# The maximum pass of the last graph attention layer: source terms fetched as bf16 parts and laid under the targets by selector products

## The reference, cut to what matters

```python
def _L3_gnn_ref(feat, src, dst, W, attn_l, attn_r):        # n = 3125, HEADS = 4, OUT_DIM = 64
    ft = (feat @ W.T).reshape(n, HEADS, OUT_DIM)
    a1 = jnp.einsum('nhd,hd->nh', ft, attn_l)
    a2 = jnp.einsum('nhd,hd->nh', ft, attn_r)
    e = jax.nn.leaky_relu(a1[src] + a2[dst], negative_slope=ALPHA)
    m = jax.ops.segment_max(e, dst, num_segments=n)
    ex = jnp.exp(e - m[dst])
    s = jax.ops.segment_sum(ex, dst, num_segments=n)
    a = ex / s[dst]
    msg = ft[src] * a[:, :, None]
    return jax.nn.elu(jax.ops.segment_sum(msg, dst, num_segments=n).reshape(n, HEADS * OUT_DIM))
```

## Time and profile before

| | |
|---|---|
| median of the runs | 6750.23 us (3 runs, 6729.89 to 6758.26) |
| the profiled execution's own time | 6752.3 us |
| its span | 6750.5 us |
| granted TensorE clock over the span | 0.812 |
| busy share PE, PEld, DVE, ACT, POOL | 69%, 45%, 57%, 32%, 51% |
| first and last gather of the maximum pass | 5400.6 and 6036.2 us |

### The profile page before, as it was taken

How to read it: one execution, slowest core, us unless ns; L and a number is a source line. 1 busy time by engine, 2 the same in 40 slices (tenths; PEclk the granted TensorE clock), 3 DMA queues, 4 the chain that set the end, 5 groups by cost and what they waited for, 6 DMA issues and landing times. The chain is left out here.

```text
span 6750.5 us, 92101 instructions
## 1 busy us (share of the span) xinstructions
PE 4675.7 (69%) x21663; PEld 3026.9 (45%) x21663; DVE 3880.6 (57%) x14947; ACT 2148.6 (32%) x7478; POOL 3474.4 (51%) x3739
## 2 busy tenths in 40 slices
PE   3566674747895555638767774778778478888858
PEld 3223333737882222424345553555567233336635
DVE  8676543130016666351578877777532667778875
ACT  0000000212231222302344444444223188874421
POOL 3636665446635666456556663666122166656610
PEclk9776656869996776955689997999788699989978
DMA  1133335546745666013155555777456166664410
GB/s 47 48 98 91 91 92 159 185 143 218 232 149 151 181 181 175 14 45 103 49 151 162 148 145 152 237 237 236 133 150 170 45 173 171 172 154 141 140 44 20
DMA packets 526133, 916.95 MB, mean 136 GB/s; under 512 B 100305, under 2 KB 382880, under 8 KB 517168
## 3 DMA queue, kind: packets, MB, share of 16 engines
q0 software_dynamic: 170800, 477.35, 26.0%
q1 hardware_dynamic: 294378, 305.07, 14.5%
q10 hardware_dynamic: 60438, 128.64, 6.0%
HBM read 739.33 MB, written 171.37 MB: 135 GB/s over the span
## 5 line engine op out<-in xcount | busy, mean ns | idle before, releaser
L999 PE MATMUL bank<-small 128*125 128x256 f32 x1660 | 763.2, 587 | 472.3 <-DVE small L966 239.9
L947 POOL DMA_INDIRECT small<-tabA,idxD x830 | 809.9, 976 | 441.0 <-issue 187.2
L999 PEld LDWEIGHTS bank<-small 128*125 128x125 f32 x1660 | 368.1, 268 | 866.6 <-issue 469.5
L978 DVE TENSOR_TENSOR big<-big,bank 125x256 f32 x830 | 347.1, 418 | 490.4 <-PE bank L999 312.6
L2506 POOL DMA_INDIRECT small<-tabC,idxD x415 | 394.5, 951 | 343.2 <-issue 124.5
L2559 PE MATMUL bank<-small 128*125 128x512 f32 x830 | 474.6, 656 | 127.1 <-issue 104.0
L2548 ACT ACTIVATE small<-cst,small 128x128 f32<-128x128 f32 x1660 | 532.2, 388 | 94.0 <-issue 40.0
L1342 DVE COPY small<-bank 128x256 f32<-128x256 f32 x176 | 74.5, 424 | 834.5 <-PE bank L1382 423.2
L2277 POOL DMA_INDIRECT big<-tabB,idxD x415 | 394.6, 951 | 300.1 <-PE bank L2340 133.6
L2091 POOL DMA_INDIRECT small<-tabT,idxS x415 | 396.5, 955 | 284.5 <-PE bank L1989 141.2
L781 POOL DMA_INDIRECT recs<-pkS,rowS x391 | 383.8, 982 | 249.4 <-issue 100.2
(11 more groups left out here) (463 smaller groups left out, 11371.0 us busy)
## 6 DMA issues: line engine op xcount, KB each, us to landing
small<-eaS SPq DMA_DIRECT2D x830, 128.0 KB
big<-in_L_w ACTq DMA_DIRECT2D x56, 1024.0 KB
eaS<-small SPq DMA_DIRECT2D x415, 128.0 KB
big<-in_L2f_w ACTq DMA_DIRECT2D x64, 512.0 KB
ytab<-small ACTq DMA_DIRECT2D x176, 128.0 KB
big<-rowsS SPq DMA_DIRECT2D x52, 256.0 KB
small<-rowsD SPq DMA_DIRECT2D x52, 256.0 KB
small<-tabA,idxD POOLq DMA_INDIRECT x830
```

The source lines that it names most:

```text
L947: g.indirect_dma_start(out=self.gb[k % self.RG], out_offset=None, in_=K.tabA, in_offset=row_index(K.idxD, k)).then_inc(*self.got.up(k))
L978: v.tensor_tensor(rows, rows, K.bank[k % 4][0:PT, 0:D], ALU.add).then_inc(*self.added.up)
L999: p.matmul(self.K.bank[k % 4][0:PT, 0:D], self.oh[k % self.RO][:, 0:PT], self.gb[k % self.RG], start=True, stop=True).then_inc(*self.summe ...
```

## The change

The four source terms of a node no longer reach the maximum pass as fp32 numbers to be spread on diagonals. `L3Project` splits each into three bf16 parts whose sum is the fp32 number, and puts these 12 parts in 6 extra columns (PW = 6) ahead of the features, in the same rows. It does so in five batches of five node tiles (`part`, four dependent VectorE operations a batch); SyncE now waits for the batch (`parted`) instead of for the node tile (`stored`), so that the stores of `tabC` go out five at a time. The rows of `tabC` grow from 260 to 266 numbers. `L3Project` also builds a constant `sel` once: for head h it is 1 in rows h, h+4 and h+8, in 128 columns.

In the maximum pass TensorE transposes the first 128 bf16 columns of the gathered rows (L2590 of the new code). Rows 0 to 11 of the result are the parts of the 128 edges; ScalarE copies these 12 rows to `rowT` (L2580), whose other rows were zeroed once. Four bf16 products of 128 columns with `sel` (L2600) lay the sum of a head's three parts under every target, on top of the product of `no` with 1e30 (L2597), which now comes first. The mask `oh` and the diagonals are gone. ScalarE still puts the a1 aside (L2581). Banks 0 to 4 are now a ring of five for the products, banks 5 to 7 one of three for the transposes; `no` is a ring of five, `rowT` one of three. GpSimd waits for `taken` in place of `spread`. The number of gathers (415) and of feature writes (415) stays.

The diff:

```diff
--- before.py
+++ after.py
@@ -136,7 +136,7 @@
-        self.tabC = self.dram("tabC", [N, AW])
+        self.tabC = self.dram("tabC", [N, CW])
@@ -2393,6 +2393,8 @@
 AW = D + 4
 WA = D + 8
+PW = 6
+CW = PW + AW
 class L3Project(Project):
@@ -2401,8 +2403,12 @@
     def __init__(self, K):
         W, g = K.W, K.g
         K.w_at = K.g_at = 0
-        self.acc, self.ft = W(T * AW), W(T * WA)
-        self.a12, self.am = self.ft.rearrange("p (t c) -> p t c", c=WA)[:, :, D:WA], W(T * 8)
+        self.acc, self.ft = W(T * AW), W(T * (PW + WA))
+        self.ftv = self.ft.rearrange("p (t c) -> p t c", c=PW + WA)
+        self.a12, self.am = self.ftv[:, :, PW + D:PW + WA], W(T * 8)
+        self.left = W(T * 4)
+        self.sel = W(256, BF16)
+        self.sel1 = W(4)
         self.am3 = W(T * 12, BF16)
         self.A1 = W(EP * 4)
         self.identB = W(64, BF16)
@@ -2417,6 +2423,7 @@
         self.t_w, self.t_wn, self.t_at = K.ticket(), K.ticket(), K.ticket()
         super().__init__(K, T)
         self.attn, self.joined = K.mark(1), K.mark(1)
+        self.parted = K.mark(T // 5)
         self.tabs = K.ring(4, T)
     def sync(self, s):
@@ -2425,8 +2432,8 @@
         load(s, self.t_wn, self.wn, a["L3_Wn"])
         load(s, self.t_at, self.bd, a["L3_attn"])
         for t in range(T):
-            s.wait_ge(*self.stored.n(t + 1))
-            s.dma_start(K.tabC[t * PT:(t + 1) * PT, :], self.ft[0:PT, t * WA:t * WA + AW]).then_inc(*self.tabs.up(t))
+            s.wait_ge(*self.parted.n(t // 5 + 1))
+            s.dma_start(K.tabC[t * PT:(t + 1) * PT, :], self.ftv[0:PT, t, 0:CW]).then_inc(*self.tabs.up(t))
         for t in range(T - 4, T):
             s.wait_ge(*self.tabs.n(t))
@@ -2445,9 +2452,31 @@
         for h in range(4):
             v.tensor_scalar(self.bigI4[:, h * 128:(h + 1) * 128], K.ident, BIG, None, ALU.mult)
         v.memset(self.acc[0:PT, :], 0.0)
+        v.tensor_tensor(self.sel1, K.ident[:, 0:4], K.ident[:, 4:8], ALU.add).then_inc(*own.up)
+        v.wait_ge(*own.all)
+        v.tensor_tensor(self.sel1, self.sel1, K.ident[:, 8:12], ALU.add).then_inc(*own.up)
+        v.wait_ge(*own.all)
+        v.tensor_copy(self.sel.rearrange("p (h e) -> p h e", h=4), self.sel1.unsqueeze(2).broadcast_to([128, 4, 128]))
         self.stats.vector(v)
-        for t in range(T):
-            self.normalize(v, t)
+        for t in range(T + 4):
+            if t < T:
+                self.normalize(v, t)
+            if t >= 8 and t % 5 == 3:
+                self.part(v, t // 5 - 1)
+
+    def part(self, v, b):
+        own, ts = self.K.own_v, slice(5 * b, 5 * b + 5)
+        a1 = self.ftv[0:PT, ts, PW + D:PW + AW]
+        parts = self.ft.bitcast(BF16).rearrange("p (t c) -> p t c", c=2 * (PW + WA))[0:PT, ts, 0:12]
+        left = self.left.rearrange("p (t h) -> p t h", h=4)[0:PT, ts, :]
+        v.wait_ge(*self.stored.n(5 * b + 5))
+        v.tensor_copy(parts[:, :, 0:4], a1).then_inc(*own.up)
+        v.wait_ge(*own.all)
+        v.tensor_tensor(left, a1, parts[:, :, 0:4], ALU.subtract).then_inc(*own.up)
+        v.wait_ge(*own.all)
+        v.tensor_copy(parts[:, :, 4:8], left).then_inc(*own.up)
+        v.wait_ge(*own.all)
+        v.tensor_tensor(parts[:, :, 8:12], left, parts[:, :, 4:8], ALU.subtract).then_inc(*self.parted.up)
     def scalar(self, a):
         K = self.K
@@ -2457,7 +2486,7 @@
                 t = i - 2
                 p = K.bank[2 + t % 2][0:PT, 0:WA]
                 a.wait_ge(*self.product.n(t + 1))
-                a.activation(self.ft[0:PT, t * WA:(t + 1) * WA], p, ACT.Copy).then_inc(*self.stored.up)
+                a.activation(self.ftv[0:PT, t, PW:PW + WA], p, ACT.Copy).then_inc(*self.stored.up)
             if i < T:
                 self.turn(a, i)
@@ -2485,52 +2514,56 @@
 class L3Max:
-    RG = 8
+    RG, RT, RN = 8, 3, 5
     def __init__(self, K, proj):
         self.K, self.pr = K, proj
         g = K.g
         K.w_at, K.g_at = proj.w_end, 0
-        self.oh, self.no = [g(128) for _ in range(4)], [g(64, BF16) for _ in range(4)]
-        self.dg, self.tm = [g(512) for _ in range(4)], [g(4) for _ in range(4)]
-        self.gb = [g(AW) for _ in range(self.RG)]
+        self.no = [g(64, BF16) for _ in range(self.RN)]
+        self.tm = [g(4) for _ in range(4)]
+        self.rowT = [g(64, BF16) for _ in range(self.RT)]
+        self.gb = [g(CW) for _ in range(self.RG)]
         self.got, self.kept_rows = K.ring(self.RG, NTE, "gather"), K.ring(self.RG, NTE)
-        self.oneh, self.spread, self.field, self.top, self.kept = (K.mark(NTE) for _ in range(5))
+        self.empty = K.mark(1)
+        self.hole, self.flipped, self.turned, self.taken, self.field, self.top, self.kept = (K.mark(NTE) for _ in range(7))
     def gpsimd(self, g):
         K = self.K
         for k in range(NTE):
             if k >= self.RG:
                 g.wait_ge(*self.kept_rows.n(k - self.RG))
-                g.wait_ge(*self.spread.n(k - self.RG + 1))
+                g.wait_ge(*self.taken.n(k - self.RG + 1))
             g.indirect_dma_start(out=self.gb[k % self.RG], out_offset=None, in_=K.tabC, in_offset=row_index(K.idxD, k)).then_inc(*self.got.up(k))
     def sync(self, s):
         K = self.K
         for k in range(NTE):
             s.wait_ge(*self.got.n(k))
-            s.dma_start(K.eaS[k * 128:(k + 1) * 128, :], self.gb[k % self.RG][:, 0:D]).then_inc(*self.kept_rows.up(k))
+            s.dma_start(K.eaS[k * 128:(k + 1) * 128, :], self.gb[k % self.RG][:, PW:PW + D]).then_inc(*self.kept_rows.up(k))
         for k in range(NTE - self.RG, NTE):
             s.wait_ge(*self.kept_rows.n(k))
     def vector(self, v):
         K, pr = self.K, self.pr
         at = Offsets(K, ENG.DVE, pr.wi4, 24 * 4)
-        for i in range(3, NTE + 7):
-            if i < NTE + 3:
+        for r in self.rowT:
+            ins = v.memset(r, 0.0)
+        ins.then_inc(*self.empty.up)
+        for i in range(NTE + 4):
+            if i < NTE:
+                k = i
+                if k >= self.RN:
+                    v.wait_ge(*self.field.n(k - self.RN + 1))
+                v.tensor_scalar(self.no[k % self.RN], K.iota, K.locD[:, k:k + 1], 1.0, ALU.is_equal, ALU.subtract).then_inc(*self.hole.up)
+            if 3 <= i < NTE + 3:
                 k = i - 3
-                if k >= 4:
-                    v.wait_ge(*self.field.n(k - 3))
-                v.tensor_scalar(self.oh[k % 4][:, 0:PT], K.iota[:, 0:PT], K.locD[:, k:k + 1], None, ALU.is_equal)
-                v.tensor_scalar(self.no[k % 4][:, 0:PT], K.iota[:, 0:PT], K.locD[:, k:k + 1], 1.0, ALU.is_equal, ALU.subtract).then_inc(*self.oneh.up)
-            if 6 <= i < NTE + 6:
-                k = i - 6
                 v.wait_ge(*self.field.n(k + 1))
                 if k >= 4:
                     v.wait_ge(*self.kept.n(k - 3))
-                v.tensor_reduce(self.tm[k % 4][0:PT, 0:4], K.bank[k % 4][0:PT, :].rearrange("p (h e) -> p h e", h=4), AXX, ALU.max).then_inc(*self.top.up)
-            if i >= 7:
-                k = i - 7
+                v.tensor_reduce(self.tm[k % 4][0:PT, 0:4], K.bank[k % 5][0:PT, :].rearrange("p (h e) -> p h e", h=4), AXX, ALU.max).then_inc(*self.top.up)
+            if i >= 4:
+                k = i - 4
                 best = pr.M3[0:PT, bass.ds(at.at(k), 4)]
                 v.wait_ge(*self.top.n(k + 1))
                 if k:
@@ -2539,25 +2572,33 @@
     def scalar(self, a):
         K, pr = self.K, self.pr
+        a.wait_ge(*self.empty.n(1))
         for k in range(NTE):
-            a.wait_ge(*self.got.n(k))
-            if k >= 4:
-                a.wait_ge(*self.field.n(k - 3))
-            gb = self.gb[k % self.RG]
-            for h in range(4):
-                a.activation(self.dg[k % 4][:, h * 128:(h + 1) * 128], K.ident, ACT.Copy, scale=gb[:, D + h:D + h + 1])
-            a.activation(pr.A1[:, 4 * k:4 * k + 4], gb[:, D:AW], ACT.Copy).then_inc(*self.spread.up)
+            a.wait_ge(*self.flipped.n(k + 1))
+            if k >= self.RT:
+                a.wait_ge(*self.field.n(k - self.RT + 1))
+            a.activation(self.rowT[k % self.RT][0:12, :], K.bank[5 + k % 3].bitcast(BF16)[0:12, 0:128], ACT.Copy).then_inc(*self.turned.up)
+            a.activation(pr.A1[:, 4 * k:4 * k + 4], self.gb[k % self.RG][:, PW + D:PW + AW], ACT.Copy).then_inc(*self.taken.up)
     def tensor(self, p):
         K, pr = self.K, self.pr
-        for k in range(NTE):
-            b = K.bank[k % 4]
-            p.wait_ge(*self.oneh.n(k + 1))
-            p.wait_ge(*self.spread.n(k + 1))
-            if k >= 4:
-                p.wait_ge(*self.top.n(k - 3))
-            p.matmul(b[0:PT, :], self.oh[k % 4][:, 0:PT], self.dg[k % 4], start=True, stop=False)
-            p.matmul(b[0:PT, :], self.no[k % 4][:, 0:PT], pr.bigI4, start=False, stop=True).then_inc(*self.field.up)
+        for i in range(NTE + 2):
+            if i < NTE:
+                p.wait_ge(*self.got.n(i))
+                if i >= 3:
+                    p.wait_ge(*self.turned.n(i - 2))
```

(12 more changed lines are left out.)

## The result

The changed kernel takes 6943.4 us (median of 4 runs, 6933.9 to 6952.6); the kernel before took 6746.2 beside it. The ratio is 1.0289, 95% interval [1.0272, 1.0306]: slower, where 1% faster was forecast. The profiled execution took 6938.1 us, 185.8 more than that of before.

What follows compares the result with a forecast made beforehand. It took ScalarE as the bound in name, GpSimd 0.02 us behind. From 6752.3 us, +3.9 (stage before), -68.7 (maximum pass) and -6.6 (its end) gave 6680.9, stated as 6681; own range 6660 to 6705, wider range 6636 to 6736.

Steps and rivals of the forecast that it cites:

- Of the 83.6 us I let 15 through.: Maximum pass: GpSimd's waits for ScalarE, 83.6 us, were to fall to 15 through slack on ScalarE.
- the excess called issue: Maximum pass: GpSimd's idle time called issue beyond 0.30 us a time, 23.4 us, expected to stay.
- GpSimd's own 551.9 us: Maximum pass: 517.5 us at GpSimd's bare 1.25 us step, plus 34.4 us of its own pauses and issue excess.
- TensorE's time: Maximum pass: 0.61 us a tile at full clock, 0.08 per small product; 1.08 us at 1.2 GHz.
- loads that don't hide: Rival, chance 0.06: in the maximum pass small products step by 0.22 us with loads in series; 6804 us.
- The clock: Rival, chance 0.18: TensorE at 1.2 GHz in half of the maximum pass, 50 of 83.6 us pass through; 6723 us.
- ScalarE and VectorE: Maximum pass: ScalarE's two small copies at most 0.56 us a tile, from 1.27; VectorE some 0.9 us left.
- DMA: Maximum pass: the same bytes in less time, DMA engines 69% busy from 62%; not a bound.
- The ends: Stage before the maximum pass +3.9 us, of it last batch +1.0 and five stores +1.8; end of the pass -6.6 us.
- The sum itself: Whole kernel: 6752.3 + 3.9 - 68.7 - 6.6 = 6680.9 us against the profiled execution, stated as 6681.

Runs made afterwards that it cites:

- tables back: Changed kernel with two floats of padding ahead of the three offset tables, so they lie at a multiple of 16 bytes again; ratio 1.0054 to the kernel before.
- tables off: Kernel before with two floats of padding ahead of the offset tables, putting them 8 bytes off a multiple of 16; ratio 1.0233.
- off by 16 bytes: Kernel before with four floats of padding ahead of the offset tables, which stay at a multiple of 16 bytes; ratio 1.0003.
- the comparison that doesn't count: Changed kernel without transposes, products on zero rows: plain transfers for gathers, 5842.1 us; GpSimd filling a tile after each gather, 6189.4; kernel before beside them 5969.4.
- the gathers alone: Changed kernel, tables moved back, maximum pass without VectorE's and TensorE's work; gathers, write-outs and ScalarE's small copy remain; 6671.5 us, gathers 567.5 us.
- TensorE cut loose from the gathers: Changed kernel, tables moved back, no transposes or ScalarE copy of the parts, products on zero rows; 6964.2 us with 10 loads and products a tile; also tried with 4.

## Why the prediction was wrong

**What was missing: the tables.** The sum went from the maximum pass straight to the end and put the sum stage behind it at no change; its +164 us are 88% of the loss. The diff showed the cause, new columns and buffers allocated ahead of the three tables, while the stage's own code stayed as it was. This is shown from both sides: tables back takes the stage from 550.9 to 386.2 us, tables off from 387.1 to 544.7, and off by 16 bytes leaves it at 386.5. In series 26 loads at 2.51 us more and 26 at 2.70 would be 135 us; that the rest comes from each engine's load making its partners wait in turn is a guess.

**"Of the 83.6 us I let 15 through."** This is the step of the maximum pass that failed; even with the tables back the kernel is 0.5% slower (1.0054), where 1% faster was forecast. In the prediction's own terms the waits for ScalarE are 131.8 - 78 x 0.30 = 108 us, where 83.6 were to fall to 15, and the excess called issue is 133.5 - 336 x 0.30 = 33 for 23.4. I read ScalarE's pauses as ScalarE's, and slack on ScalarE as their cure. With ScalarE's work cut to 0.33 us a tile at the old count of loads and products the pass was 631.3 us for 635.6. The runs show another cause: VectorE and ScalarE wait for TensorE's semaphores, which come late beside the gathers and writes. What is let through, put as the pass less 567.5, is 68 us before and 91 with the change. It grows with TensorE's loads and products, which the change doubled from 6 to 12 a tile: taking 6 of the 12 away again gives back 24 and 26 us. My reading of the ring is that GpSimd's buffers come free only through TensorE's semaphores, so that a full ring stops the gathers and the semaphores then come, and more slack or more buffers only put that off. This is inferred from the pauses that end while GpSimd stands; a stand of GpSimd was tried by itself only in the comparison that doesn't count. Why a semaphore is late at all is open, and so is the jump from 567 to 628 at four loads and products with little between four and eight.

**GpSimd's own 551.9 us** (517.5 + 34.4) were 16 too few, and with the 15 let through they met the gathers alone (567.5) by chance. Part of the 16 are the waits for feature writes, which the prediction had at nothing.

**TensorE's time was right.** Four small products at full clock, in the changed kernel:

```profile
5704.76 0.39 PE L2600 MATMUL bank<-small,big 128*128 128x128 bf16 x4
5704.98 0.22 PE L2590 MATMUL bank<-big,small 128*128 128x128 bf16 x1
```

The four products and their four loads take 0.22 us until the next start, 0.055 each, below the 0.08 I took. So it was luck of the rival "loads that don't hide" that the result fell on its side: its step of 0.22 us for a small product is not there, and the measured time beyond its 6804 has another cause. The rule of the Trainium skill weighed then stands on the page "TensorE: Matmul & The Clock Gate" in the section "The mechanism", not in the one that the prediction names: a load overlaps running products only if its row groups differ. This row disagrees with it, as rows 7 did. The same section also lets a load go ahead into the background weight buffer, which the prediction left out and which this row doesn't speak against.

**The clock** fell to 0.66 in the pass, as the rival said. It did not decide by what there is: of the two kernels with tables back that differ by three small products, the one at the lower clock (0.51 for 0.69) had the shorter pass (631.3 for 657.1), and with no gathers beside, a stream of 4 loads and products at 0.50 kept VectorE's pace. The changed kernel itself was not run at full clock.

**ScalarE and VectorE** came as worked out: ScalarE 136 us in the pass, 0.33 a tile (the bound was 0.56), VectorE 367 us, 0.90 a tile (0.9).

**DMA** stood at 60% for the forecast 69, since the pass got no shorter; the gathers alone had 69%.

**The ends.** From the last store of `ft` to the first gather 9.6 us pass (5387.2 to 5396.8) for 4.4; +5.2 where the last batch and the five stores together were to cost 2.8. The first gather still starts 3.8 us earlier, since all that lies ahead of that store was 9.0 us shorter in this execution, for a reason that is open. The end of the pass gained 0.7 us for the forecast's 6.6, presumably by late semaphores too.

**The sum itself** has a slip: 6680.9 against the profiled execution is 6679 against the median, not 6681. It changes nothing.

## What to carry to other kernels

A new buffer moves all that is allocated behind it. Look at what other instructions read there by address, above all tables that engines load into registers, and keep them on a multiple of 16 bytes, as both fast places here were; check unchanged stages first when a change costs more than its own stage could. Slack pays only if what fills it doesn't cost the engine that is truly late: ask of a pause whose semaphore ended it, and whether its product was long over in the record. Where indirect gathers run beside TensorE, as in this pass, count its loads and products a tile as well as their time. And when two streams seem to go one for one, look at single steps before believing it: here the totals matched within 1% (410 and 406) and the steps showed two separate beats.

## What was not expected of the hardware

- Loading 16 offsets into the registers of VectorE or TensorE takes 1.10 us from a table at a multiple of 16 bytes and 3.60 (VectorE) or 3.80 us (TensorE) from one 8 bytes off. Other offsets than 8 and 16 were not tried.
- Beside back-to-back indirect gathers and their write-outs, what waits for TensorE is released up to 12 us after the products are over in the record. In two runs with TensorE cut loose from the gathers this went at an even 1.40 us for each load or product (14.00 us for 10, 5.60 for 4), and it went on for at least 5.1 and 7.1 us after the last gather was issued, while transfers still ran. Without gathers beside, there was no delay (0.6 us in 415 tiles).
- One comparison ran the whole kernel before in 5969 us, once, and two variants beside it showed no such delays.
